# Attention rebuilt with the values as the stationary operand, and the division and output projection moved into the feed-forward kernel

## The reference

```
q, k = rmsnorm(x @ Wq), rmsnorm(x @ Wk)         # per head, over 64 channels
gate = softplus(einsum(k, u_n) / 8)             # one number per key and head
bias = -max(i - j, 0) * omega_eff[h] * gate[j]  # -inf above the diagonal
attn = softmax(q k^T / 8 + bias)
x    = layernorm(x + (attn @ v) @ Wproj)
h    = silu(x W1') * (x W2'); h = gelu(h H1'); h = gelu(h H2')
out  = layernorm(x + h W3')
```

## Time and profile before

| | |
|---|---|
| median of 3 runs | 3840.42 us (3836.8 to 3847.71) |
| profiled execution, its own time | 3829.98 us |
| its span, first to last instruction | 3828.2 us |
| PE busy | 3582.7 us |
| DVE, ACT, POOL busy | 1931.5, 1408.1, 469.8 us |
| DMA moved | 137.66 MB, 36 GB/s on average |

### The profile page before, as it was taken

The page is one execution under the profiler, slowest core; times in us unless marked ns, Lnnn a source line. Parts: engine busy times, 40 slices in busy tenths (PEclk is TensorE's granted clock), DMA queues, the critical chain, the costliest instruction groups (busy, mean ns, idle before and its releaser), DMA issues. The chain is left out here.

```text
span 3828.2 us, 58077 instructions
## 1 busy us (share of the span) xinstructions
PE 3582.7 (94%) x23600; PEld 3206.4 (84%) x23600; DVE 1931.5 (50%) x4396; ACT 1408.1 (37%) x2367; POOL 469.8 (12%) x290
## 2 busy tenths in 40 slices
PE   3799999999999999999999999999899999899999
PEld 2698888988888898888889888898778888778887
DVE  3556666556665655666655666656233122133232
ACT  1244444444444444444444344444333232232222
POOL 3112111112111111211111211111000000000000
PEclk9899999999999999999999999999899999999999
DMA  1110011110001111001110001110121111130110
GB/s 54 34 26 20 21 22 28 27 23 21 20 21 30 44 37 54 21 20 26 27 27 21 20 21 25 28 25 17 52 87 36 53 45 50 45 128 34 66 67 17
DMA packets 116121, 137.66 MB, mean 36 GB/s; under 512 B 39568, under 2 KB 72464, under 8 KB 115856
## 3 DMA queue, kind: packets, MB, share of 16 engines
q1 hardware_dynamic: 115856, 133.96, 13.0%
HBM read 54.22 MB, written 29.36 MB: 22 GB/s over the span
## 5 line engine op out<-in xcount | busy, mean ns | idle before, releaser
L766 PEld LDWEIGHTS ps_v<-values,exps 128*128 128x128 f32 x8704 | 1133.2, 192 | 146.8 <-ACT exps L478 78.5
L766 PE MATMUL ps_v<-values,exps 128*128 128x65 f32 x8704 | 1149.8, 272 | 48.2 <-DVE y_tok L684 45.2
L478 ACT ACTIVATE exps<-ps_s,bias 128x512 f32<-128x512 f32 (+3 forms) x1280 | 797.5, 623 | 869.2 <-PE ps_s L754 555.9
L666 DVE TENSOR_REDUCE maxes<-ps_m 128x1 f32<-128x512 f32 x768 | 529.1, 689 | 313.4 <-PE ps_m L802 305.0
L802 PE MATMUL ps_m<-k_ext,q_max 128*128 128x512 f32 (+3 forms) x1280 | 538.4, 434 | 59.5 <-DVE maxes L666 56.3
L753 PE MATMUL ps_s<-q_twice,k_split 128*128 128x512 f32 (+3 forms) x1280 | 496.7, 388 | 0.0
L754 PE MATMUL ps_s<-q_ext,k_ext 128*128 128x512 f32 (+3 forms) x1280 | 470.3, 367 | 0.0
L663 DVE CUSTOM_DVE_ANT_0 ps_m<-ps_m,mask_row 128x128 f32<-128x128 f32 (+3 forms) x512 | 254.1, 496 | 244.4 <-PE ps_m L802 242.2
L729 PE MATMUL ps_p<-w_hi,xt_hi 128*128 128x194 f32 x1024 | 294.3, 287 | 25.6 <-POOL w_lo L411 20.3
L802 PEld LDWEIGHTS ps_m<-k_ext,q_max 128*128 128x128 f32 x1280 | 241.6, 195 | 82.7 <-issue 47.7
L488 ACT ACTIVATE raw<-ps_p 128x386 f32<-128x386 f32 x256 | 126.2, 493 | 438.7 <-PE ps_p L729 438.7
(11 more groups left out here) (186 smaller groups left out, 5391.8 us busy)
## 6 DMA issues: line engine op xcount, KB each, us to landing
q_twice<-q_max SPq DMA_DIRECT2D x256, 128.0 KB, 2.3
k_split<-k_ext SPq DMA_DIRECT2D x128, 128.0 KB, 2.2
hidden<-gelu SPq DMA_DIRECT2D x64, 256.0 KB, 2.0
a_in<-hidden SPq DMA_DIRECT2D x8, 2048.0 KB, 10.5
x_rows<-in_L_attn_x_dram SPq DMA_DIRECT2D x16, 256.0 KB, 2.9
acc<-in_L_attn_x_dram SPq DMA_DIRECT2D x2, 2048.0 KB, 9.9
attended<-acc SPq DMA_DIRECT2D x8, 512.0 KB, 2.9
x_tok<-attended SPq DMA_DIRECT2D x8, 512.0 KB, 4.0
```

The costliest lines, as they stand in the source:

```text
L478: nc.scalar.activation(exps[:, u_ % PR, off:QB], ps_s[u_ % 2][:, off:QB], ACT.Exp, bias=bias[slot][:, kt, qb:qb + 1]).then_inc(ex_done, 1)
L666: nc.vector.tensor_reduce(maxes[:, qt, kc:kc + 1], ps_m[v % 2][:, 0:width], AX.X, ALU.max).then_inc(mx_free, 1)
L766: last = nc.tensor.matmul(ps_v[:, t * (D + 1):(t + 1) * (D + 1)], exps[:, u_ % PR, t * P:(t + 1) * P], values[second][:, kt, :], start=(kt ...
```

## The change

In attention the values become the stationary operand (`v_main`, `v_rest`, 66 columns) and the exponentials move through, 512 queries at a time. Each unit has a mode (`mode_of`). In modes P and D ACT takes the exponential twice, once rounded into `e_hi` and once in full into `e_all`; POOL (mode P, 26 of 40 units) or DVE (mode D, 6) subtracts them into `e_lo` (`take_rest`, L329); PE makes three rounded passes, two of them two units after the scores (L843, L845) and the third, with `e_lo`, four units after (L854, step "values rest"). The two narrowest units of each group (mode F, 8 per head) stay in full float32, one product each (L838). The result stands with channels on partitions, in two banks; DVE copies it to `y_out` (L736), and SP writes it undivided, with the row sums, to DRAM (`yt`). The sums are read back, inverted (L740) and written as `recip_sums`.

Projection, squares, powers, norms and gates are made for two heads at once, in smaller steps (16 projection steps of 392 columns, eight squares, eight powers of 128x8, eight norms). The maxima reach `q_ext` by one transpose of four columns (L802) and a DMA. `attention_steps` writes one list for all 32 heads. `ffn_up` now loads y and the reciprocals, POOL multiplies them (L1056), ACT and DVE split the product (L1089, L1146), PE multiplies it with `Wproj` (L1236, `project_y`), and x is added before the norm (L1153).

```diff
+NBIAS = 4
+KCOLS = D + NBIAS
+CK = 2 * D
+CV = CK + 2 * KCOLS
+WCOLS = CV + 2 * D
...
-LAG = 2
+LAG, LAG_LO = 2, 4
...
+E_RING, HI_RING, LO_RING, Q_RING = 3, 4, 3, 3
...
+def mode_of(v):
+
+
+    qb, kt = UNITS[v]
+    if kt - TQ * qb >= TQ // 2:
+        return "F"
+    return "D" if kt < TQ * qb and kt % TQ == TQ - 1 else "P"
...
+    for p in range(PAIRS):
+        t0 = 2.0 * p
+        at(t0 - 2.60, "load", p)
+        at(t0 - 2.40, "weights", p)
+        for t in range(TT):
+            at(t0 - 1.68 + 0.036 * t, "project", p, t)
+        for i in range(8):
+            at(t0 - 1.09 + 0.025 * i, "square", p, i)
+        at(t0 - 0.88, "mean", p)
+        for i in range(8):
+            at(t0 - 0.87 + 0.025 * i, "power", p, i)
+        at(t0 - 0.66, "gate a", p)
+        at(t0 - 0.64, "gate exp", p)
+        for i in range(8):
+            at(t0 - 0.63 + 0.01 * i, "norm", p, i)
+        for i in range(GATE_PARTS):
+            at(t0 - 0.55 + 0.01 * i, "gate b", p, i)
...
+        if LAG <= u < HEADS * NU + LAG:
+            steps.append(("values", *divmod(u - LAG, NU)))
+        if u >= LAG_LO:
+            n, v = divmod(u - LAG_LO, NU)
+            if MODES[v] != "F":
...
+        def take_rest(eng, on, n, v):
+
+            u_ = NU * n + v
+            qb, kt = UNITS[v]
+            off = max(0, kt - TQ * qb) * P
+            i = count_of("PD", u_)
+            eng.wait_ge(hi_done, i + 1)
+            eng.wait_ge(ex_done, u_ + 1)
+            if i >= LO_RING:
+                eng.wait_ge(pv_lo, i + 1 - LO_RING)
+            on.tensor_tensor(e_lo[:, i % LO_RING, off:QB], e_all[:, u_ % E_RING, off:QB],
+                             e_hi[:, i % HI_RING, off:QB].bitcast(F32), ALU.subtract).then_inc(lo_by[MODES[v]], 1)
...
+                if step[0] == "square":
+                    p, i = step[1:]
+                    col, rows = (0, D, k_cols(0), k_cols(1))[i // 2], slice(i % 2 * HT, (i % 2 + 1) * HT)
+                    gp.wait_ge(pj_free, TT * (p + 1))
+                    if p or i >= 4:
+                        gp.wait_ge(ss_done, 8 * p + i - 3)
+                    nc.gpsimd.tensor_tensor(sq[:, i % 4, :, :], raw[:, rows, col:col + D], raw[:, rows, col:col + D], ALU.mult).then_inc(sq_done, 1)
+                if step[0] == "power":
+                    p, i = step[1:]
+                    rows = slice(i % 2 * HT, (i % 2 + 1) * HT)
+                    gp.wait_ge(ms_done, p + 1)
+                    nc.gpsimd.tensor_tensor(rs[:, i // 2, rows], mean_sq[:, i // 2, rows], power[:, rows], ALU.pow).then_inc(rs_done, 1)
...
+                if step[0] == "values":
+                    n, v = step[1:]
+                    if MODES[v] == "P":
+                        take_rest(gp, nc.gpsimd, n, v)
...
-                        nc.scalar.activation(exps[:, u_ % PR, off:QB], ps_s[u_ % 2][:, off:QB], ACT.Exp,
-                                             bias=bias[slot][:, kt, qb:qb + 1]).then_inc(ex_done, 1)
+                    if MODES[v] != "F":
+                        i = count_of("PD", u_)
+                        if i >= HI_RING:
+                            before = split_units[i - HI_RING]
+                            act.wait_ge(pv_hi, before + 1)
+                            rest_taken(act, before)
+                        nc.scalar.activation(e_hi[:, i % HI_RING, off:QB], ps_s[u_ % 2][:, off:QB], ACT.Exp, bias=by).then_inc(hi_done, 1)
+                    if u_ >= E_RING:
+                        before = u_ - E_RING
+                        if MODES[before % NU] == "F":
+                            act.wait_ge(pv_hi, before + 1)
+                        else:
+                            rest_taken(act, before)
+                    nc.scalar.activation(e_all[:, u_ % E_RING, off:QB], ps_s[u_ % 2][:, off:QB], ACT.Exp, bias=by).then_inc(ex_done, 1)
...
+                if step[0] == "norm":
+                    p, i = step[1:]
+                    col, rows = (0, D, k_cols(0), k_cols(1))[i // 2], slice(i % 2 * HT, (i % 2 + 1) * HT)
+                    glink(nc.vector.tensor_tensor(raw[:, rows, col:col + D], raw[:, rows, col:col + D],
+                                                  rs[:, i // 2, rows].unsqueeze(2).broadcast_to([P, HT, D]), ALU.mult))
...
-                        nc.vector.reciprocal(recip[:], pv[:, :, D]).then_inc(rc_done, 1)
-                        dve.wait_ge(rc_done, NQB * n + qb + 1)
-                        nc.vector.tensor_tensor(y_tok[:, qb * TQ:(qb + 1) * TQ, second * D:(second + 1) * D],
-                                                pv[:, :, 0:D], recip[:].unsqueeze(2).broadcast_to([P, TQ, D]), ALU.mult).then_inc(y_done, 1)
+                if step[0] == "take":
+                    n, qb = step[1:]
+                    grp = n * NQB + qb
+                    dve.wait_ge(pv_hi, units_before(n, qb))
+                    dve.wait_ge(pv_lo, count_of("PD", units_before(n, qb)))
+                    if grp >= 2:
+                        dve.wait_ge(y_out_done[grp % 2], 16 * (grp // 2))
+                    nc.vector.tensor_copy(y_out[:, grp % 2, :], ps_v[grp % 2][0:D + 1, :]).then_inc(y_done, 1)
...
-                        for t in range(TQ):
-                            col = neg_max[:, qb * TQ + t:qb * TQ + t + 1]
-                            last = nc.tensor.matmul(ps_t[:, t * P:(t + 1) * P], col.broadcast_to([P, P]), ident_r[:],
-                                                    start=True, stop=True)
+                    nc.tensor.transpose(ps_t[0:VCOLS, 0:P], neg_max[:, qb * TQ:qb * TQ + VCOLS], ident[:]).then_inc(tr_full, 1)
...
-                        for t in range(max(0, kt - TQ * qb), TQ):
-                            last = nc.tensor.matmul(ps_v[:, t * (D + 1):(t + 1) * (D + 1)],
-                                                    exps[:, u_ % PR, t * P:(t + 1) * P],
-                                                    values[second][:, kt, :],
-                                                    start=(kt == 0 and t == 0), stop=(kt == TQ * qb + t),
-                                                    skip_group_check=True)
-                        last.then_inc(pv_done, 1)
+                    if MODES[v] == "F":
+                        pe.wait_ge(ex_done, u_ + 1)
+                        nc.tensor.matmul(bank[0:VCOLS, off:QB], v_full[s][:, kt // TQ, kt % TQ - TQ // 2, :], e_all[:, u_ % E_RING, off:QB],
+                                         start=False, stop=kt == TQ * (qb + 1) - 1, skip_group_check=True).then_inc(pv_hi, 1)
+                    else:
+                        i = count_of("PD", u_)
+                        pe.wait_ge(hi_done, i + 1)
+                        nc.tensor.matmul(bank[0:VCOLS, off:QB], v_main[s][:, kt, :], e_hi[:, i % HI_RING, off:QB], start=kt == 0, stop=False,
+                                         skip_group_check=True)
+                        nc.tensor.matmul(bank[0:VCOLS, off:QB], v_rest[s][:, kt, :], e_hi[:, i % HI_RING, off:QB], start=False, stop=False,
+                                         skip_group_check=True).then_inc(pv_hi, 1)
+                if step[0] == "values rest":
+                    n, v = step[1:]
+                    u_, s = NU * n + v, n % 2
+                    qb, kt = UNITS[v]
+                    off = max(0, kt - TQ * qb) * P
+                    i = count_of("PD", u_)
+                    rest_taken(pe, u_)
+                    nc.tensor.matmul(ps_v[(n * NQB + qb) % 2][0:VCOLS, off:QB], v_main[s][:, kt, :], e_lo[:, i % LO_RING, off:QB],
+                                     start=False, stop=kt - TQ * qb == TQ // 2 - 1, skip_group_check=True).then_inc(pv_lo, 1)
+
...
+        def load_y(sp, i, c):
+            m = OC * i + c
+            if m >= YR:
+                sp.wait_ge(ylo_done, m + 1 - YR)
+            if m >= 2:
+                sp.wait_ge(y_scaled, m - 1)
+            tok = slice(i * NTOK % T, i * NTOK % T + NTOK)
+            for j in range(2):
+                head = i * NTOK // T * H + 2 * c + j
+                sp.dma_start(y_in[j * D:(j + 1) * D, m % YR, :], yt_dram[head, 0:D, tok]).then_inc(y_load[m % YR], 16)
+                sp.dma_start(r_in[j * D:(j + 1) * D, m % 2, :], recip_dram[head, tok].partition_broadcast(D)).then_inc(y_load[m % YR], 16)
...
+            def first_x(i):
+                for m in range(OC * i, OC * (i + 1)):
+                    gp.wait_ge(y_load[m % YR], 64 * (m // YR + 1))
+                    nc.gpsimd.tensor_tensor(y_in[:, m % YR, :], y_in[:, m % YR, :], r_in[:, m % 2, :], ALU.mult).then_inc(y_scaled, 1)
...
+            def project_y(i, c):
+                m = OC * i + c
+                pe.wait_ge(ylo_done, m + 1)
+                if c == 0:
+                    pe.wait_ge(wp_done, 2)
+                    pe.wait_ge(l1_free, 2 + OC * i)
+                for t in range(NT):
+                    out = ps_1[t // 2][:, t % 2 * C:(t % 2 + 1) * C]
+                    tok = slice(t * P, (t + 1) * P)
```

(7 more changed lines are left out.)

1192 lines of the change are left out of this document (614 added, 578 removed).

## The result

The changed kernel takes 3963.9 us (median of 4 runs, 3961.75 to 3966.1), against 3844.07 us (4 runs) for the kernel before beside it: a ratio of 1.031 (95% interval 1.030 to 1.033), slower. The forecast was 3746 with a range from 3500 to 3930. The profiled execution took 3966.1 us.

What follows compares the result with a forecast made beforehand. PE was taken to bound the kernel: 157 + 32 x 64.0 - 26 + 255 + 122 = 2556; plus 9, 582 + 104, 483 and 2 gives 3736, and 10 for median over profile 3746 us; range 3500 to 3930.

Steps and rivals of the forecast that it cites:

- (a) to (c): Attention, squares and powers, norms and gate, turns: POOL and DVE fall behind and stop PE, 17 us per pair, 255.
- (b): Norm and gate stretch, 0.25 head: DVE needs 16.7 us against PE's 10.6, so 6 us per pair.
- (c): Turns stretch, 0.25 head: POOL needs 18.1 us against 16.4, 2 us per pair plus 1 for four weight steps.
- The other waits, 3.8 per head: Attention's remaining small waits and bubbles of PE: 3.8 us per head, 122 us, bounds 0 and 6.5 per head.
- PE's work, 64.0 per head: Attention: PE's own passes, priced by spacing, fall from 74.3 to 63.0 us per head, 64.0 with the clock.
- rival D: Values product: 66-row passes run slower and gain nothing, +4.3 us per head, 3884 us; chance 0.04 within B's share.
- Start, 157: Start of attention, one pair prepared before scores: 157 us for 160, bounds 135 and 180.
- First feed-forward kernel, 104 more: First feed-forward kernel: added projection passes 11.2 us per block, 90, plus 14 in the first block; bounds 85 and 130.
- A (slack swallows it): Attention: PE stays the bound, slack and free tiles swallow the POOL and DVE backlog: 3491 us; chance 0.25.
- C (ACT): Attention: ACT binds because two exponentials per tile cost their full 0.69 us each: 3790 us; chance 0.08.
- B: Gate chain: DVE's steps each wait for POOL on their shared path, 36 us, total 4061 us; chance 0.22 with D.

Runs made afterwards that it cites:

- no_subtract: The changed kernel without the subtractions that make e_lo (all 32 per head); the third values pass stays and reads a constant: 3602.6 us, ratio 0.938.
- stops_in_even_heads: no_subtract with 128 stops of PE, each waiting for one POOL power, put into the even heads where POOL has nothing else to do: 3941.7 us.
- no_subtract_later: no_subtract with the first head's turns, bias and value copies of each pair 0.06 head later: 3580.8 us, ratio 0.933.
- stops_alone: no_subtract with 128 stops of PE, each waiting for one POOL power, put into the odd heads: 3944.2 us, ratio 1.027.
- ends_mended: The changed kernel with constant fills after the first w_in copy, first projection on two banks, earlier y splits and y loads in feed-forward: 3895.0 us.
- slack_one_tile: The changed kernel with one more slot in rings e_all, e_hi and e_lo, and the third pass one unit later: 3979.9 us, ratio 1.036.

## Why the prediction was wrong

**Direction.** It named the right place, the stretch from squares to turns where POOL and DVE stop PE, but took PE's savings to be larger than its price, and gave slower 0.23. The sum missed by 230 us on the span: 142 in the main part, 48 and 35 at its ends.

**The step that failed: (a) to (c), "In all 17 us per pair", 255 in all.** By its own terms 222 of this were for the subtractions, and no_subtract measured 363: this one term is the miss of the main part. The step took a stop of PE to cost its own length. Of the 363, 198 are idle time of PE, less than the 222, so the length was not put too low. On top come 91 of clock loss (138 against 47), which no term held: the prediction multiplied PE's work by the mean clock of the kernel before, 0.984, though it was forecasting 17 us of new stops per pair. And on top come 74 more of busy time, which I read as the run-out and the slow restart at each stop.

stops_in_even_heads shows that ratio with stops put in one by one: 343 us for 227 of stops, 1.5, or 1.4 by PE's whole idle time. In the change it is 363 / 198 = 1.8, which these stops do not reach; what makes the change's own stops dearer stays open.

**(b) alone.** DVE's chain was put at 16.7 us and took 20.8. The one norm at 0.65 is 0.71 undisturbed, 1.31 beside POOL's subtractions. Not counted was what stands behind it: DVE's own subtractions are queued there, and PE stands for them.

**(c) alone.** Put at 2 to 3 us per pair, it took 5.4. Over the 15 pairs PE's idle time in this stretch grew by 34 us, under the 45 forecast; another 45 us of clock loss come on top of it.

**The other waits, 3.8 per head.** 2178 - 2022 = 156 us for 122 + 33 = 155: held in size. In part this is luck, since the wait of a pair's first turn for the gate chain brings clock loss that no term tied to it: 33 of no_subtract's 47 us went with that wait in no_subtract_later.

**PE's work, 64.0 per head.** Held: 66-column passes start 0.23 apart, so rival D falls, and PE's busy time less the clock loss is 2009 us in no_subtract against 1990 (63.0 per head). The turning with 68 stationary columns is between the bounds 0.110 and 0.058: four take 0.36 us in PE's timeline of stops_alone, 0.09 each, some 20 us less in all than with 0.110. The prediction's estimate of 57 ns from the Trainium skill, "TensorE: Matmul & The Clock Gate", section "LDWEIGHTS (loading the stationary operand)", is not reached.

```profile
1107.37 0.60 PE L792 MATMUL ps_t<-ident,raw 128*68 128x128 f32 x4
1107.73 0.31 PE L827 MATMUL ps_s<-q_twice,k_split 128*128 128x128 f32 x1
```

**Start, 157.** It was 192.4. DVE's fills lie in line ahead of the first weights, and the projection's passes start 0.33 us apart there, not 0.18, so its sixteen steps took 2.9 us each, not 1.9. PE's timeline:

```profile
78.53 0.53 PE L774 MATMUL ps_p<-w_lo,xt_hi 128*128 128x392 f32 x1
78.85 0.53 PE L774 MATMUL ps_p<-w_hi,xt_lo 128*128 128x392 f32 x1
```

ends_mended took 50 us of this away by order and a second bank alone; with the two banks the passes are 0.18 apart after the first few steps.

**First feed-forward kernel, 104 more.** It was 152. A block grew by 19.7 us, from 65.9 to 85.6, not by 11.2 (the prediction's 72.7 per block had the kernel's opening spread over the eight). PE waits in each block: 3.55 us for DVE's split of a tile of y. In ends_mended, where DVE splits it earlier, PE waits 1.65 us instead, for another DVE step, the clock loss of seven blocks falls from 19 us to 3, as much as before the change, and a block takes 3.4 us less. With the 1.65 that stay, some 3.5 us per block are left that I can't place.

**Rivals.** A (slack swallows it) is refuted by PE's idle time from squares to powers, 96 us in the 15 pairs, 6.4 each, where the prediction put A's limit at 5, and by slack_one_tile; C (ACT) by no_subtract. B named the shared path of DVE and POOL: it is there, and every small DVE step of the chain that started beside a POOL instruction waited, but POOL runs dry when PE stops, as the prediction's argument against B said, and the chain grew by 8.7 us per pair, not by 36. What it gives PE by itself was not separated from POOL's queue.

## What to carry to other kernels

Where an engine that feeds TensorE in order falls behind, add to the length of the stops what the clock and the restart take: here a stop of 1.77 us cost 2.7, and 3.5% of the span (138 of 3964 us) was clock loss in attention. Look for the stretch where the feeding engine is full on end, not for its share of the span: POOL was busy for 44%. There a saving on one of its loads mostly hands the stop to the next engine in line; leaving the extra work out in that stretch alone, with a costlier product on PE that needs no subtraction, brought nearly all of it back (292 of 333 us).

## What was unexpected of the hardware

- Stops of one length (1.77 us) are followed now by 392-column passes 0.18 us apart and now by passes 0.33 apart; the clock did not simply follow the longest stops.
- The small DVE steps of the gate chain that started while POOL ran were held up each time (75 of 75 took 0.9 us or more, the 255 others 0.36 at most). What limited the harm was how often POOL had something to run.
- In the first 200 us of the profile the column PEclk says 1.00 while the projection's passes are 0.33 apart, where at 2.4 GHz elsewhere they are 0.18. The spacing is what counts.
- One POOL power over 8 columns takes 1.64 us; eleven small DVE steps, a shift, a subtraction and three Newton steps of three instructions each, replace eight of them in 3.7 us.
